# Pair-sum transfers of a half issued ahead of GpSimd's adds, in an attention and int8 FFN kernel

## The reference

```python
Q, K, V = (proj(Wq), proj(Wk), proj(Wv))            # einsum('oc,bct->bto'), C = 512, T = 1024
att = jnp.einsum('bhqd,bhkd->bhqk', Q, K) * (1.0 / math.sqrt(Dh)) + b[0]
att = att * m + (1.0 - m) * NEG_INF
y = jnp.einsum('bhqk,bhkd->bhqd', jax.nn.softmax(att, axis=-1), V)
y = y.transpose(0, 2, 1, 3).reshape(B, T, C).transpose(0, 2, 1)
q, in_scale = per_token_quant_int8(y)                # rows of 1024
acc = jnp.einsum('bsk,nk->bsn', q, weight, preferred_element_type=jnp.int32)
out = x + (acc.astype(float32) * in_scale * w_scale[:, 0] + bias).astype(float16)
```

## Time and profile before

| | us |
|---|---|
| median of 3 runs | 2414.33 (2413.55 to 2414.71) |
| profiled execution | 2414.74 |
| its span, first to last instruction | 2412.8 |

### The profile page before, as it was taken

One profiled execution on the slowest core, in us unless ns is written; L12 is line 12 of the kernel. 1 busy time (PEld: TensorE's weight loads), 2 busy tenths in 40 slices (PEclk: granted clock), 3 DMA queues, 4 the chain that ended last, 5 costly groups with the idle time before them and its releaser, 6 DMA issues.

```text
span 2412.8 us, 36511 instructions
## 1 busy us (share of the span) xinstructions
PE 2342.3 (97%) x11840; PEld 1320.4 (55%) x11872; DVE 1561.4 (65%) x1683; ACT 1343.3 (56%) x2536; POOL 1725.1 (71%) x740
## 2 busy tenths in 40 slices
PE   8999999999999999999999999999999999999996
PEld 7888888885444444444444444444444444444442
DVE  3311111147787777777787877777778777787771
ACT  3322222215666666666666666666666666666664
POOL 3322233324888888888888888888888888888887
PEclk9999999999999999999999999999999999999998
DMA  6645554467888888898988998888988888989971
GB/s 244 255 187 216 200 200 184 175 213 165 194 185 194 193 191 199 195 195 196 203 194 191 195 194 193 190 188 191 196 195 184 197 190 195 201 193 194 204 151 47
DMA packets 152569, 462.60 MB, mean 192 GB/s; under 512 B 15592, under 2 KB 51432, under 8 KB 128304
## 3 DMA queue, kind: packets, MB, share of 16 engines
q0 software_dynamic: 27216, 198.19, 42.9%
q10 hardware_dynamic: 48864, 129.19, 20.5%
q1 hardware_dynamic: 76416, 134.34, 15.5%
HBM read 161.51 MB, written 100.93 MB: 109 GB/s over the span
## 4 chain that ended last, share of the span: by engine, by line
PE 77%; DMA 10%; POOL 5%; issue 3%; ACT 2%; ACTq 1%; SPq 1%; DVE 1%; POOLq 0%; DVEq 0%
PE score L725 18%; PE pv L754 16%; PE ring L131 15%; PE ring L324 11%; PE score L324 9%; DMA q_stack<-max_lo 8%; PE ring L788 4%; POOL acc L1026 4%; PE pv L324 3%; PE ring L769 1%; ACT probs L836 1%; DMA k_stack<-bias_part 1%; ACTq L119 1%; DMA probs<-probs 1%; PE ring L779 1%
## 5 line engine op out<-in xcount | busy, mean ns | idle before, releaser
L836 ACT ACTIVATE probs<-score 128x512 f32<-128x512 f32 x2048 | 1076.8, 604 | 590.6 <-PE score L725 539.8
L140 DVE TENSOR_REDUCE neg_max<-ring 128x1 f32<-128x1024 f32 x1024 | 1210.8, 1220 | 260.3 <-PE ring L131 251.8
L725 PE MATMUL score<-q_stack,k_stack 100*128 100x512 f32 x2048 | 878.1, 430 | 36.4 <-DMA q_stack<-max_lo 21.1
L1026 POOL TENSOR_TENSOR acc<-acc,probs 128x2048 f32<-128x2048 f32 x189 | 876.8, 4639 | 21.5 <-DMA probs<-probs 12.9
L131 PE MATMUL ring<-k_stack,q_stack 98*128 98x512 f32 x2048 | 811.4, 396 | 2.8 <-DMA k_stack<-bias_part 1.8
L725 PEld LDWEIGHTS score<-q_stack,k_stack 100*128 100x128 f32 x2048 | 386.1, 189 | 530.1 <-ACT probs L836 370.9
L754 PE MATMUL pv<-probs,v_in 128*32 128x512 f32 x4096 | 546.3, 605 | 0.0
L131 PEld LDWEIGHTS ring<-k_stack,q_stack 98*128 98x128 f32 x2048 | 389.3, 190 | 73.4 <-DVE neg_max L140 6.8
L1026 POOL TENSOR_TENSOR acc<-probs 128x2048 f32<-128x2048 f32 x63 | 288.7, 4582 | 191.5 <-DMA probs<-probs 121.9
L526 POOL TENSOR_TENSOR q_stack<-x_raw,k_stack 128x1024 fp32r<-128x1024 f32 x28 | 67.7, 2455 | 292.2 <-ACT k_stack L402 292.2
L1010 POOL DMA_DIRECT2D probs<-probs x189 | 172.8, 914 | 52.2 <-PE pv L754 48.8
(11 more groups left out here) (101 smaller groups left out, 1950.0 us busy)
## 6 DMA issues: line engine op xcount, KB each, us to landing
probs<-probs POOLq DMA_DIRECT2D x189, 1024.0 KB, 9.1
q_stack<-qk_part ACTq DMA_DIRECT2D x183, 256.0 KB, 7.9
k_stack<-qk_part ACTq DMA_DIRECT2D x90, 512.0 KB
qk_part<-part_hi SPq DMA_DIRECT2D x64, 512.0 KB, 2.6
qk_part<-part_lo SPq DMA_DIRECT2D x64, 512.0 KB, 3.5
v_steps<-v_out SPq DMA_DIRECT2D x64, 256.0 KB, 2.2
v_out<-x ACTq DMA_DIRECT2D x32, 512.0 KB, 5.6
out<-v_out SPq DMA_DIRECT2D x64, 256.0 KB, 2.0
```

What stands on the lines that cost most here:

```text
L140: nc.vector.tensor_reduce(neg_max[:, pair // CHUNK, pair % CHUNK:pair % CHUNK + 1], ring[:, :], AX_X, ALU.max, negate=True).then_inc(neg_m ...
L725: pe.matmul(score[score_bank(t)][:, :], k_stack[par][0:ROWS, h, kt * P:(kt + 1) * P], q_stack[par][0:ROWS, half, h, :], start=True, stop=T ...
L836: nc.scalar.activation(probs[:, kt, h, :], score[score_bank(t)][:, :], ACT.Exp).then_inc(exp_done, 1)
L1026: nc.gpsimd.tensor_tensor(acc[:, half, :, :], first, probs[:, tile, :, :], ALU.add).then_inc(acc_done, 1)
```

## The change

The tile pairs are others: the transfers now add tile 0 into 1, 3 into 2 and 5 into 4, and POOL adds 1 + 2, then 6, 4 and 7. Add 0 therefore reads the targets of pairs 0 and 1 and waits for both; before, it read tile 4 and the target of pair 0. In POOL's order the adds move behind the transfers of their half: in half 0 the three pairs (with the two normalise operations between and behind them) and then adds 0 to 3; in half 1 pairs 0 and 1, finish 0, pair 2, finish 1, add 0, and adds 1 to 3 at the head of the next step, ahead of that step's pair 0. The numbers of transfers and adds and the work of all other engines are the same.

```diff
-PAIRS_OF_TILES = ((0, 1), (2, 3), (6, 5))
-FIRST, ADDED = 4, (1, 3, 7, 5)
+PAIRS_OF_TILES = ((0, 1), (3, 2), (5, 4))
+FIRST, ADDED = 1, (2, 6, 4, 7)
@@ add(s, half, k)
                 if k == 0:
-                    pool.wait_ge(exp_done, UNITS * s + GH * (half * TT + FIRST + 1))
+                    pool.wait_ge(pair_done[SUMMED_BY[FIRST]], 16 * (halves_before(s, half) + 1))
                     wait(pool, sum_done, halves_before(s, half) - 1)
@@ step(s, par, prev=True, main=True, ahead=True)
                 if prev and main:
-                    begin_pair(s, 0, 0)
-                    add(s - 1, 1, 3)
-                elif main:
+                    for k in range(1, ADDS):
+                        add(s - 1, 1, k)
+                if main:
                     begin_pair(s, 0, 0)
                 if prev:
                     normalise(s - 1, 0)
                 if main:
                     begin_pair(s, 0, 1)
-                    add(s, 0, 0)
+                    begin_pair(s, 0, 2)
                 if prev:
                     normalise(s - 1, 1)
                 if main:
-                    begin_pair(s, 0, 2)
-                    for k in range(1, 4):
+                    for k in range(ADDS):
                         add(s, 0, k)
                 if main and ahead:
                     begin_pair(s, 1, 0)
                     begin_pair(s, 1, 1)
-                    add(s, 1, 0)
 ...
                 if prev:
                     finish(s - 1, 1)
                 if main and ahead:
-                    for k in range(1, 3):
-                        add(s, 1, k)
+                    add(s, 1, 0)
```

## The result

The changed kernel takes 2610.98 us (median of 4 runs, 2609.03 to 2611.93) beside 2414.52 us: a ratio of 1.0812, 95% interval 1.0793 to 1.0831. The forecast was 2595 us, its range 2505 to 2665. The profiled execution lasted 2609.03 us, its span is 2607.2 us.

A forecast was written before the change was run, and what follows sets the result against it. The prediction took POOL's loop, adds plus exposed landings of second pair transfers, to bound the changed kernel: 31 loops of 63.1 us move the end by 180.6 us from 2414.7, giving 2595 us, range 2505 to 2665.

The forecast's parts named there:

- The bound after the change: POOL's loop of adds and exposed pair transfers sets the step: 63.1 us, bounds 61.1 and 65.3, against 57.16 before.
- The terms of the sum: One POOL loop: 32.5 us to pair 0 of half 1, then 11.8 landing, 0.2 start, 18.5 adds, together 63.1 us.
- Normalise 1 and the factor: In half 0, normalise 1 waits for DVE's factor behind the row sums; costed at nothing, with 13 us of cover.
- the idle of 6 to 10 us: POOL's idle ahead of the block of four adds in half 0, expected to be ended by the pair transfer.
- PE will stand there about 6 us in each step.: At tile 1 of half 1, exponentials wait for add 0, so PE stands about 6 us each step.
- rival A: Transfer queue is worse: later pair landings or row maxima held back; loop above 64.4 us, 2636 to 2690 us; chance 0.14.
- D: TensorE's clock may halve after 6 us stalls; held hidden in PE's standing time; no chance of its own, counted in rival A.
- POOL with its transfers is a loop about as long as PE's own step: In the kernel before, POOL's loop of 56.8 us matches the 57.16 us step; only about 1 us covers a longer one.
- C, overlap of close transfers: Second pair transfers land as if alone: loop 56.5 us, 2395 us; chance 0.06 faster, 0.03 within 0.2%.
- The Trainium skill's price: For pair transfers: 2.0 us plus bytes over 436 GB/s, some 4.4 us for 1 MB; loop would be about 51 us.

The follow-up runs named there:

- experiment 1: The changed kernel with add 0 taking tiles 1 and 6 and add 1 tile 2, so the first add no longer needs pair 1: 2524.76 us.
- experiment 3: The changed kernel with 12 extra matmuls ahead of PE's wait for the row maxima at slot 32: 2615.15 us.
- experiment 7: The kernel before with the changed kernel's tile pairs but its own old order of POOL: 2923.85 us, ratio 1.2095.
- experiment 4: The kernel of experiment 1 with 12 extra matmuls ahead of PE's wait for the row maxima at slot 32: 2485.95 us.
- experiment 11: The kernel before, tile pairs kept, with pair 0 of half 1 issued ahead of add 3 of half 0 and finish 1 ahead of pair 2: 2418.19 us.
- experiment 6: The changed kernel's order with the tile pairs of the kernel before, add 0 needing only pair 0: 2561.16 us, ratio 1.0595.

## Why the prediction was right, and where it was not

*The bound after the change.* Right. POOL's loop with two exposed second landings sets the time: experiment 1 takes the exposure away and 86 us go, experiment 3 adds PE work and only 4 us are lost, experiment 7 exposes more and the step grows by 16.3 us over the 57.16 of before, where 17.8 had been foreseen.

*The terms of the sum.* In half 0 pair 1 landed 14.05 us behind the issue of pair 0 (13.8 forecast), and in half 1 add 0 began 12.05 us behind it (12.0). The adds were 18.5, the loop 63.15. The agreement in half 0 is in part luck: two errors cancel. The first landing took 8.3 us in the median and not 8.9, and the second came 5.8 us behind it and not 4.9. The 16 us that the median is above 2595 are small terms: 31 x 0.16 = 5 for the loop's mean of 63.26; 6 for the first add 0, at 584.7 and not 578.5, since pair 1 of the first step landed only 14.3 us after its issue at 570.32; 2.5 for the tail, 61.3 us from the last add 0 to the end where I had 58.8; and 2 by which the median is above the profiled execution.

*Normalise 1 and the factor,* costed at nothing with a cover of 13 us. Right for the sum, but the cover was smaller: in the step shown the factor came 8.2 us behind pair 0, and POOL stood 3.89 us for it (112.8 us in 29 waits). That wait took the first part of the idle of 6 to 10 us that I had expected to end with the pair transfer; 4.67 us of it were left, and the landing still came last.

*"PE will stand there about 6 us in each step."* Wrong in place. Only 38.9 us of ACT's waits end with POOL's add. PE stands earlier, at slots 32 and 0, for row maxima, and behind most of the longer of these gaps it loses the clock for a stretch. I had this as a part of rival A and of D, and had counted it as lying within the 6 us. That held for the sum, as experiment 3 shows. What I did not see is how nearly it filled them: with POOL's waits gone (experiment 1) the kernel is still at 2525 us, so that 110 of 197 us are lost twice over.

*D, the clock.* That it would fall was right; that it costs nothing was right only under POOL's loop: without that loop experiment 4 prices it at some 39 us. The page of the Trainium skill that I named, TensorE: Matmul & The Clock Gate, section "HAM oscillation — how this bites in real kernels", describes a kernel whose waits for transfers, of some 3 to 5 us, each have a slow stretch behind them. The trace agrees in kind, but here shorter gaps did it, as 0.53 of full speed behind 2.76 us shows, and not every time.

*"POOL with its transfers is a loop about as long as PE's own step."* The length was right, and the conclusion for the new loop held, but in experiment 11 fewer waits of ACT for POOL's adds gave nothing. Most of these 30.3 us lay in slack.

*C, overlap of close transfers,* is refuted: 5.85 and 5.3 us between landings for issues 1.85 and 1.6 us apart. The Trainium skill's price that the prediction weighed, some 4.4 us for 1 MB, does not hold for these accumulating transfers, since the least landing here is 6.9 us.

## What to carry to other kernels

When an in-order engine issues transfers and then waits for their sums, write its loop down: work, plus for each block the time to the landing of the *last* transfer that the first consumer needs, less what is placed in between. Give the first consumer the data that lands first, and put the next in later; here the two orders of the same four adds differ by 86 us. Then look for the second bound before believing in a gain: here small transfers that PE waits for were delayed by bulk ones of two other queues, and moving one bulk load away from their slot was worth more (10 us of 2415) than easing POOL's order in the same kernel (experiment 11, nothing).

## What the runs showed of the hardware that was not expected

- An accumulating transfer of 1 MB inside SBUF landed 6.9 us after its issue at the least. Issued while another was on its way, it landed behind that one by 5.1 us (median, 4.9 to 5.9) in half 1, where pair 1 is issued 0.6 us behind pair 0, and by 5.8 us (4.4 to 6.9) in half 0, with more loads beside it.
- The 8 KB stores of row maxima landed 2.1 to 7.3 us after their issue in the steps of the kernel before, and 5.8 to 9.0 us in the changed one.
- The counts here are of PE's gaps in the steps that began at full clock. In the changed kernel TensorE fell to 1.2 GHz within 4 us behind 22 of the 28 gaps of 2.5 us and more, and behind 5 of the 24 between 1.25 and 1.75 us. In the kernel of experiment 6 it did so behind 29 of 34 gaps of this shorter kind. So a short gap is no assurance, and the length of the gap alone does not tell; why these two kernels differ stays open.
- Filling the gap at slot 32 with useless matmuls made the kernel of experiment 1 39 us faster, and the changed kernel not at all.
